# Another order of the operations in each step of a two-layer Mamba scan, on all four compute engines

## What is computed

```python
for i in range(2):
    u = layernorm(h)
    z, xBC, dt = split(u @ in_w.T)                 # 512, 640, 8
    dt = softplus(dt + dt_bias)
    xh, Bm, Cm = split(silu(causal_conv4(xBC)))    # 512, 64, 64
    state = exp(dt * A) * state + (dt * x_t) * B_t # scan over time, 8 heads
    y = state @ C_t + D * xh
    y = rmsnorm(y * silu(z)) @ out_w.T
    h = y + h
```

## Time and profile before

| | |
|---|---|
| median of 3 runs | 1979.9 us (1978.9 to 1980.2) |
| span of the profiled execution | 1980.0 us |
| PE busy | 1819.1 us, 92% |
| DVE busy | 1534.9 us, 78% |
| ACT busy | 1260.0 us, 64% |
| POOL busy | 1189.5 us, 60% |
| granted PE clock, mean over the span | 0.969 of full |

### The profile page before, as it was taken

One profiled execution on the slowest core, in us unless ns is written; L12 is line 12 of the kernel. 1 busy time (PEld: TensorE's weight loads), 2 busy tenths in 40 slices (PEclk: granted clock), 3 DMA queues, 4 the chain that ended last, 5 costly groups with the idle time before them and its releaser, 6 DMA issues. The chain is left out here.

```text
span 1980.0 us, 36525 instructions
## 1 busy us (share of the span) xinstructions
PE 1819.1 (92%) x12544; PEld 1380.2 (70%) x12544; DVE 1534.9 (78%) x3311; ACT 1260.0 (64%) x2221; POOL 1189.5 (60%) x1032
## 2 busy tenths in 40 slices
PE   5899999999999999999999999999974798988898
PEld 4577776777777777677777776777753677777776
DVE  4777888878778877777777777777635799999986
ACT  3677767776777666777677767777720455555554
POOL 2566666667666655555555555555540687868785
PEclk8899999999999989999999999999985899999999
DMA  4011111111111101111111111110005202012001
GB/s 141 22 39 38 39 48 58 37 42 37 37 37 37 48 28 49 59 39 44 37 37 37 37 48 58 37 42 26 28 11 148 86 1 95 34 41 89 33 12 43
DMA packets 87271, 91.96 MB, mean 46 GB/s; under 512 B 4928, under 2 KB 82448, under 8 KB 87184
## 3 DMA queue, kind: packets, MB, share of 16 engines
q1 hardware_dynamic: 79360, 79.46, 12.4%
q10 hardware_dynamic: 7824, 11.37, 2.3%
HBM read 57.26 MB, written 25.17 MB: 42 GB/s over the span
## 5 line engine op out<-in xcount | busy, mean ns | idle before, releaser
L860 POOL TENSOR_TENSOR L_xc<-L_xpad,L_vec 128x512 f32<-128x512 f32 x160 | 166.2, 1039 | 420.6 <-ACT L_xpad L659 401.3
L381 PE MATMUL L_front<-L_uhi,L_whi 128*128 128x512 f32 x576 | 247.2, 429 | 10.7 <-DVE L_xc L1078 7.3
L530 PE MATMUL L_mix<-L_wo,L_yg 128*128 128x256 f32 x1024 | 238.8, 387 | 3.2 <-POOL L_yg L852 3.2
L381 PE MATMUL L_front<-L_uhi,L_wlo 128*128 128x512 f32 x576 | 229.7, 399 | 0.0
L381 PE MATMUL L_front<-L_ulo,L_whi 128*128 128x512 f32 x576 | 229.7, 399 | 0.0
L1090 DVE TENSOR_TENSOR L_m<-L_dbank,L_gm 128x512 f32<-128x512 f32 x256 | 175.4, 685 | 69.6 <-ACT L_dbank L699 69.1
L530 PEld LDWEIGHTS L_mix<-L_wo,L_yg 128*128 128x128 f32 x1024 | 192.1, 193 | 35.0 <-issue 7.2
L852 POOL TENSOR_TENSOR L_yg<-L_yg,L_sz 128x512 f32<-128x512 f32 x128 | 164.3, 1284 | 85.9 <-DVE L_yg L1105 85.9
L659 ACT ACTIVATE L_xpad<-L_front,L_pbias 128x512 f32<-128x512 f32 x160 | 108.8, 681 | 131.8 <-PE L_front L381 130.9
L697 ACT ACTIVATE L_dbank<-L_dbank 128x512 f32<-128x512 f32 x256 | 148.8, 581 | 46.7 <-PE L_dbank L437 46.6
L1619 POOL TENSOR_TENSOR M_alo<-M_hT,M_ahi 128x512 fp32r<-128x512 f32 x96 | 125.6, 1312 | 75.1 <-DVE M_ahi L1681 75.1
(11 more groups left out here) (174 smaller groups left out, 4912.5 us busy)
## 6 DMA issues: line engine op xcount, KB each, us to landing
h<-L_hres SPq DMA_DIRECT2D x32, 512.0 KB, 3.0
L_hin<-in_x SPq DMA_DIRECT2D x16, 512.0 KB, 4.6
L_hres<-in_x SPq DMA_DIRECT2D x16, 512.0 KB, 3.8
L_cc<-L_xc ACTq DMA_DIRECT2D x64, 128.0 KB, 2.3
L_hin<-h SPq DMA_DIRECT2D x16, 512.0 KB, 4.7
L_hres<-h SPq DMA_DIRECT2D x16, 512.0 KB, 3.8
M_hin<-h SPq DMA_DIRECT2D x16, 512.0 KB, 6.4
M_xin<-in_x SPq DMA_DIRECT2D x16, 512.0 KB, 6.7
```

The source lines that it names most:

```text
L381: last = nc.tensor.matmul(to[:, :], ww[:, kd, tile * P:(tile + 1) * P], a[:, kd, :], start=i == 0, stop=i == len(passes) - 1)
L530: last = nc.tensor.matmul(mix[1 - s][:, (b % 2) * DM:(b % 2 + 1) * DM], yg[:, t, b * P:(b + 1) * P], wo[layer][:, t, :], start=t == 0, sto ...
L860: nc.gpsimd.tensor_tensor(xc[p][:, q, :].rearrange("p (b i) -> p b i", b=NB), xpad[:, q, :, 0:P], vector(layer, "conv_w", q * TAPS, 1).uns ...
```

## The change

The lines inside the four `step` functions change places. The instructions themselves, their waits and their buffers stay, with one exception: the wait for the cleared halo, which clear_halo did at once, is now done by the next set_halo that copies from it.

The hunks up to line 620 are PE's step, those from 749 to 802 ACT's, from 884 to 915 POOL's, and from 1169 on DVE's.

```diff
@@ -562,6 +562,6 @@
                     project_conv(n + 1, 0)
-                turn_x(n, p, 0)
+                decays(n, 4)
                 if more:
                     turn_dt(n + 1)
-                decays(n, 4)
+                turn_x(n, p, 0)
                 if follows_any(n):
@@ -571,5 +571,5 @@
                 turn_x(n, p, 1)
-                turn_x(n, p, 2)
                 decays(n, 5)
                 decays(n, 6)
+                turn_x(n, p, 2)
                 turn_x(n, p, 3)
@@ -587,9 +587,10 @@
                 outputs(n, p, 1)
-                outputs(n, p, 2)
                 if more:
                     project_conv(n + 1, 4)
-                    sum_da(n + 1)
                 new_state(n, 0)
-                new_state(n, 1)
+                outputs(n, p, 2)
+                if more:
+                    sum_da(n + 1)
                 outputs(n, p, 3)
+                new_state(n, 1)
                 if more:
@@ -600,5 +601,5 @@
                     project_z(n + 1, 3)
+                    scores(n + 1, 1 - p)
                     decays(n + 1, 0)
                     decays(n + 1, 1)
-                    scores(n + 1, 1 - p)
                 if more2:
@@ -606,5 +607,2 @@
                 result(n, layer, 0)
-                if more:
-                    decays(n + 1, 2)
-                    decays(n + 1, 3)
                 square_sums(n)
@@ -612,4 +610,8 @@
                     fold_bias(layer_of(n, layer, 2))
+                if more:
+                    decays(n + 1, 2)
                 if more2:
                     project_dt(n + 2)
+                if more:
+                    decays(n + 1, 3)
 
@@ -749,5 +751,4 @@
                     keep_dt(n + 1)
-                exp_decay(n, 3)
-                if more:
                     raw_conv(n + 1, layer1, 1 - p, 0)
+                exp_decay(n, 3)
                 exp_decay(n, 4)
@@ -757,2 +758,4 @@
                 exp_decay(n, 6)
+                if more:
+                    raw_conv(n + 1, layer1, 1 - p, 2)
                 keep_b(n)
@@ -761,4 +764,2 @@
                 exp_decay(n, 7)
-                if more:
-                    raw_conv(n + 1, layer1, 1 - p, 2)
                 exp_carry(n, 2)
@@ -766,5 +767,4 @@
                 if more:
-                    softplus(n + 1)
                     raw_conv(n + 1, layer1, 1 - p, 3)
-                    silu_conv(n + 1, layer1, 1 - p, 0)
+                    softplus(n + 1)
                 if more2:
@@ -772,21 +772,27 @@
                 if more:
-                    silu_conv(n + 1, layer1, 1 - p, 1)
-                    double_c(n + 1, 1 - p)
-                    silu_conv(n + 1, layer1, 1 - p, 2)
                     raw_conv(n + 1, layer1, 1 - p, 4)
+                    keep_halo(n + 1, 1 - p)
+                    silu_conv(n + 1, layer1, 1 - p, 0)
+                    double_c(n + 1, 1 - p)
+                    silu_conv(n + 1, layer1, 1 - p, 1)
                 square(n, 0)
-                square(n, 1)
-                square(n, 2)
                 if more:
+                    silu_conv(n + 1, layer1, 1 - p, 2)
                     silu_conv(n + 1, layer1, 1 - p, 3)
+                square(n, 1)
+                if more:
                     silu_z(n + 1, layer1, 0)
-                    keep_halo(n + 1, 1 - p)
+                square(n, 2)
+                if more:
                     silu_z(n + 1, layer1, 1)
-                    silu_conv(n + 1, layer1, 1 - p, 4)
                     silu_z(n + 1, layer1, 2)
                     silu_z(n + 1, layer1, 3)
-                    exp_decay(n + 1, 0)
                 square(n, 3)
                 if more:
-                    exp_decay(n + 1, 1)
+                    silu_conv(n + 1, layer1, 1 - p, 4)
+                    exp_sums(n + 1, 1 - p)
+                if starts_layer(n + 2):
+                    fold_weights(layer_of(n, layer, 2))
+                if more:
+                    exp_decay(n + 1, 0)
                 if more2:
@@ -794,6 +800,4 @@
                 if more:
+                    exp_decay(n + 1, 1)
                     exp_decay(n + 1, 2)
-                    exp_sums(n + 1, 1 - p)
-                if starts_layer(n + 2):
-                    fold_weights(layer_of(n, layer, 2))
 
@@ -883,3 +887,2 @@
                 twice = layer_of(n, layer, 2) == 0
-                decay_state(n, p)
                 if more:
@@ -887,5 +890,9 @@
                     first_tap(n + 1, layer1, 1 - p, 1)
-                to_end(n, p, 0)
+                if twice:
+                    model_norm(n + 2, p)
+                if more2:
+                    layer_norm(n + 2)
                 if more:
                     first_tap(n + 1, layer1, 1 - p, 2)
+                to_end(n, p, 0)
                 to_end(n, p, 1)
@@ -893,15 +900,10 @@
                     first_tap(n + 1, layer1, 1 - p, 3)
-                if more2:
-                    layer_norm(n + 2)
                 to_end(n, p, 2)
                 to_end(n, p, 3)
-                gate(n, 0)
                 if more:
                     first_tap(n + 1, layer1, 1 - p, 4)
+                decay_state(n, p)
+                gate(n, 0)
                 gate(n, 1)
-                if twice:
-                    model_norm(n + 2, p)
                 gate(n, 2)
-                if next_layer == 0:
-                    norm_residual(n + 1, c + p, 1 - p)
                 gate(n, 3)
@@ -909,6 +911,8 @@
                 add_squares(n, 2)
+                if next_layer == 0:
+                    norm_residual(n + 1, c + p, 1 - p)
                 add_squares(n, 3)
+                rsqrt(rrms, ssq, ss_done, n, rr_done)
                 if more:
                     second_operands(n + 1)
-                rsqrt(rrms, ssq, ss_done, n, rr_done)
 
@@ -1052,2 +1056,4 @@
                     dve.wait_ge(cleared, 1)
+                elif isinstance(n, int) and n % ITEMS < GROUPS:
+                    dve.wait_ge(halo_cleared, (n // ITEMS - 1) * GROUPS + g + 1)
                 nc.vector.tensor_copy(xpad[:, :, :, 0:HALO].rearrange("p q b i -> p (q b) i"),
@@ -1059,3 +1065,2 @@
                 nc.vector.memset(halo[g][:, :, :, :], 0.0).then_inc(halo_cleared, 1)
-                dve.wait_ge(halo_cleared, n // ITEMS * GROUPS + g + 1)
 
@@ -1169,2 +1174,4 @@
                 chunk2 = 0 if ends_sequence(n) else c + 1
+                if more:
+                    set_halo(n + 1, 1 - p)
                 if more2:
@@ -1172,13 +1179,11 @@
                 if more:
-                    set_halo(n + 1, 1 - p)
+                    convolve(n + 1, layer1, 1 - p, 0, 0)
                 weigh(n, 3)
-                scale_x(n, p, 0)
                 if more:
+                    convolve(n + 1, layer1, 1 - p, 0, 1)
                     bias_dt(n + 1, layer1)
-                    convolve(n + 1, layer1, 1 - p, 0, 0)
                 weigh(n, 4)
-                if more:
-                    convolve(n + 1, layer1, 1 - p, 0, 1)
                 if follows_any(n):
                     finish(n - 1, layer_of(n, layer, -1), None, 1 - p, 1)
+                scale_x(n, p, 0)
                 if more:
@@ -1204,20 +1209,22 @@
                     convolve(n + 1, layer1, 1 - p, 2, 1)
-                skip(n, layer, p, 0)
-                if more:
-                    finish_dt(n + 1, layer1, 1 - p)
                     convolve(n + 1, layer1, 1 - p, 2, 2)
                     convolve(n + 1, layer1, 1 - p, 3, 0)
+                skip(n, layer, p, 0)
+                if more:
                     convolve(n + 1, layer1, 1 - p, 3, 1)
-                    convolve(n + 1, layer1, 1 - p, 3, 2)
                 skip(n, layer, p, 1)
                 if more:
-                    split_sums(n + 1)
+                    finish_dt(n + 1, layer1, 1 - p)
+                    convolve(n + 1, layer1, 1 - p, 3, 2)
                     convolve(n + 1, layer1, 1 - p, 4, 0)
-                skip(n, layer, p, 2)
-                if more:
                     convolve(n + 1, layer1, 1 - p, 4, 1)
                     convolve(n + 1, layer1, 1 - p, 4, 2)
+                    split_sums(n + 1)
+                skip(n, layer, p, 2)
+                if more:
                     decay_operands(n + 1)
-                    first_operands(n + 1)
+                skip(n, layer, p, 3)
                 add_state(n, p, 0)
+                if more:
+                    first_operands(n + 1)
                 add_state(n, p, 1)
@@ -1225,3 +1232,2 @@
                     clear_halo(n, p)
-                skip(n, layer, p, 3)
                 if more:
@@ -1229,5 +1235,2 @@
                     weigh(n + 1, 0)
-                    weigh(n + 1, 1)
-                if starts_layer(n + 2):
-                    fold_rows(layer2)
                 if more2:
@@ -1237,3 +1240,5 @@
                 if more:
-                    weigh(n + 1, 2)
+                    weigh(n + 1, 1)
+                if starts_layer(n + 2):
+                    fold_rows(layer2)
```

(19 more changed lines are left out.)

22 lines of the change are left out of this document (10 added, 12 removed).

## The result

The changed kernel takes **1990.1 us** (1989.7 to 1991.6, four runs) against 1980.1 us for the kernel before in the same session: ratio 1.0051, 95% interval 1.0037 to 1.0065. The forecast was 1989. The profiled execution has a span of 1987.8 us, 7.8 more than before; its run took 1989.7, so a run's time lies 1.9 above its span. The text ahead of the prediction, and the prediction with it, set a span beside a median of run times and found 0.1 between them. Like with like, the profiled execution of the kernel before was a long one: 21 later runs of it had spans of 1975.6 to 1979.5, median 1977.7, against its 1980.0. So the change costs 10.1 us by the medians, where two traces show 7.8 and the prediction added up 9.3.

What follows compares the result with a forecast made beforehand. PE was taken as nearly the bound (42.96 of 44 us busy), paying for DVE's chain. Plain steps -0.5 - 0.6 + 1.3 = +0.2, times 29 = +5.8; start-up +2.0, layer change +1.5: +9.3 on 1980.0, 1989 us, range 1975 to 1997.

Steps and rivals of the forecast that it cites:

- After outputs, -0.5: Plain step, outputs to turn_cum: PE's 0.62 us wait before turn_cum goes, splitting new_state costs 0.1; sum -0.5 us.
- turn_cum to square_sums, -0.6: Plain step: decays 2 and 3 leave this stretch (0.53 us) and scores' move saves one switch; sum -0.6 us.
- Square sums to outputs, +1.3: Plain step, DVE chain: weigh 2 +0.60, set_halo held by second_operands +0.68, moments +0.4, less 0.4 us; sum +1.3.
- The moments' hold: One of moments' nine small DVE operations is held by POOL's first_tap 0: +0.4 us, bounds 0 and 1.04.
- the sentence in bold: Of the DVE chain from square sums to outputs: "Whatever is put into that chain, PE pays for.".
- My first rival: Second hold does not bite: chain +0.8 instead of +1.3, a step -0.3 us, 1976 us; chance 0.27.
- The wait before outputs: PE's 0.27 us idle before outputs waits for weigh 7, the end of the long DVE chain from the square sums.
- Start-up step, +2.0: bias_dt falls later on DVE, so project_conv 1 starts later: +2.0 us, bounds 1.0 and 4.0.
- Change of layer, +1.5: ACT rounds new weights earlier, delaying mean_square; fold_bias's wait grows from 1.33 to about 2.8: +1.5 us, bounds 0 and 3.
- Last step, 0: No next item to prepare; its waits on finish and second_operands trade places: 0 us.
- The cover that I called thin: With decay_state ahead on POOL, gates and add_squares end about 0.5 us before square_sums needs them: no cost.
- longer still: Rival: rsqrt 0.3 us later makes decays 4 wait for second_operands, 0.3 more a step, 1998 us; chance 0.12.

Runs made afterwards that it cites:

- 4: The kernel before with only the change's last third of a step (from outputs to turn_cum): 1962.6 us, ratio 0.9914.
- 6: 4 with new_state in two pieces, placed as in the changed kernel: 1964.2 us, ratio 0.9927.
- experiment 2: The changed kernel with set_halo done one step earlier, between mean_square and finish: 1978.7 us, ratio 0.9997.
- 3: The changed kernel with weigh 2 and the earlier set_halo between mean_square and finish, and weigh 3 ahead of convolve(0, 0): 1988.7 us, ratio 1.0047.
- 11: The changed kernel with moments ahead of set_halo again and weigh 3 ahead of convolve(0, 0): 1979.8 us, ratio 1.0002.
- experiment 10: The changed kernel with only moments and set_halo swapped back on DVE, moments first: 1992.3 us, ratio 1.0062.
- 7: The changed kernel with bias_dt back ahead of convolve(0, 0) on DVE and fold_weights back behind exp_decay 2 on ACT: 1989.2 us, ratio 1.0050.
- experiment 8: The changed kernel with the order of before from outputs to turn_cum on all four engines: 2026.4 us, ratio 1.0238.
- experiment 1: The changed kernel with weigh 2 back ahead of finish on DVE, nothing else: 1994.9 us, ratio 1.0079.

## Why the prediction was right, and where its reasons were not

The waits and holds that it named are in the rows. Several sizes were off, the account of the middle third left out a term, and the total came closer than its parts.

- **After outputs, -0.5**: measured -0.40 (13.72 to 13.32). The wait, 0.66 as a mean, is gone; what PE pays for it was mis-sized, some 0.25 in place of 0.1 (experiments 4 and 6: taking the wait away brings 0.55, the split takes 0.15 back).
- **turn_cum to square_sums, -0.6**: -0.57. But "scores ahead of decays 0 and 1 saves one switch" was wrong: the two together take 1.52 us, 1.42 before.
- **Square sums to outputs, +1.3**: +1.37 and +1.24. weigh 2 and set_halo's hold are in the rows with the predicted sizes, and convolve(1, 0) came at t = 25.09 (24.95 predicted). The moments' hold was mis-sized: 0.85 in the step shown where +0.4 was counted, because first_tap 0 started at t = 17.51 and not 17.1. What hid it is that the moments' nine operations began at 17.49 and not 17.7, and the ninth ended at 19.30, where the sum gives 19.05. What failed is the sentence in bold, that PE pays for whatever is put into that chain, as the account of it all. With 0.65 of the chain taken out (experiment 2) this third is still 18.78, +0.87. Decays 2 and 3 left the first third, which I counted as -0.6, and came into this one with their 0.53 us and the switches around them, which I counted nowhere. PE's own work in this third, its length less the idle time, is 18.55 there against 17.68 before, and 18.4 to 18.5 in experiments 3 and 11 with the same order on PE: +0.75 to +0.9. The third stood only 0.6 to 0.85 us above that in the changed kernel. My first rival's +0.8 would have made the third 18.7, 0.15 to 0.3 above what PE alone takes; the kernel that came nearest to it (experiment 2) ended at the time of before, not at 1976.
- **The wait before outputs**, which the prediction called the end of that chain, is 0.22 to 0.24 us as a mean over the inner steps of each of the fourteen kernels, also where the chain's head was 0.65 us shorter. So something behind convolve(0, 0) sets its length; which wait it is, no run separates.
- **The holds** explain where DVE's time goes, yet taking both away by the swap wins nothing (experiment 10), since convolve(0, 0) needs first_tap 0 in any case. The same 0.6 us are won by what is put into that time (11) or by an earlier set_halo (2).
- The Trainium skill's rule ("SBUF — State Buffer", "Who interferes with whom") agrees with the rows of after, 0.73 and 1.01 us, and with the held operations of the experiments. It doesn't agree with the COPY beside an rsqrt that took 0.19 us, shown under the hardware; there the measurement decides.
- **Start-up step, +2.0**: +3.1 (46.51 to 49.59), inside its bounds; project_conv 1 waited 3.35 us for bias_dt (the first row below). Undoing it gave 2.3 back (7). The 0.6 for a fall of PE's clock is a term that no run shows: the mean granted clock of this step was 0.88, against 0.85 before.
- **Change of layer, +1.5**: +1.0; fold_bias waited 2.55 us (2.8 predicted), the second row:
```profile
76.53 0.56 PE L381 MATMUL L_front<-L_uhi,L_whi 128*128 128x512 f32 x1 [3.35 <-DVE L_dtraw L997]
735.68 7.81 PE L353 MATMUL L_ybank<-L_vec,L_raw 128*128 128x1 f32 x36 [2.55 <-DVE L_ssq L1125]
```
- **Plain steps, +5.8**: the 29 together +8.3. The excess lies where the terms above were mis-sized.
- **Last step, 0**: from the last turn_cum to the last store it is 54.06 in place of 58.46 us, -4.4. The mean granted clock of this stretch is 0.91, against 0.85 before, and PE's busy time in it 46.3 against 48.8 us; the causes of the rest aren't separated.
- **The total**: the steps between the marks cost 12.4 us more, 9.3 were forecast. The trace of after is also 1.2 longer ahead of the first turn_cum and, behind the last one, 4.4 shorter in the last step and 1.4 in the MLP, where I had counted nothing. The trace of before has the longest such tail of all fourteen (554.4 us, the others 548.6 to 552.3). That the excess of the steps met a gain behind them, and the total so came out within 1.1 us, is in part luck.
- The wait for cleared halos and decay_state's place cost nothing that a PE row of the changed kernel shows. The cover that I called thin, POOL ahead of the square sums, was thin: experiment 8 lost 22 us to it, through norm_residual.
- The rival "longer still" did not come: decays 4 found second_operands ended (426.76 against 427.01), 0.25 us to spare.

## What to carry to other kernels

Take a change of order apart by stretches of the step before judging it: here one third was worth 16 us and the rest cost 24 (47 without the room that the third made for norm_residual), and the whole looked like a slight loss. Where work is moved off one stretch, book it at the place where it lands, on the engine that is nearly full, and add the neighbours' switches. And before an operation is moved, ask whether its old place kept two others apart: set_halo behind the moments did.

## What the runs showed of the hardware

- DVE operations of 4 to 60 elements a partition whose operands are all in SBUF (COPY, TENSOR_TENSOR, SCALAR_TENSOR_TENSOR, TENSOR_SCALAR; 0.16 to 0.20 us) take 0.5 to 1.1 us when a POOL operation of 512 or 1024 elements a partition runs, and end with it within 0.1 us, whichever of them is met (0.49 in experiment 1, 1.04 in 3, 1.10 in the earlier trace rows). The four bn_stats whose first half ran beside second_operands in experiment 2 took 1.40 us, as in the step of after, where they ran behind it.
- Not every POOL operation holds: in experiment 2 the COPY at 421.22 ran beside the rsqrt, in 0.19 us. Whether this is for its kind or for its 4 elements a partition, no run tells.
```profile
420.59 1.02 POOL L816 TENSOR_TENSOR L_rrms<-L_ssq,L_power 128x4 f32<-128x4 f32 x1 [1.77 <-DVE L_ssq L1125]
```
- A single bf16 matmul among fp32 ones costs PE some 0.1 us on either side: from the last matmul of project_dt over decays 3 to the second of project_conv 0 it takes 0.99 us with decays 3 in between, where the two matmuls without it took 0.47 in the kernel before; so 0.52 for one, against 0.53 for the pair of the earlier trace rows. The two kinds differ in type, in rows (64 and 128) and in the bank they write; no run separates these.
```profile
424.77 0.40 PE L368 MATMUL L_front<-L_uhi,L_wlo 128*8 128x512 f32 x1
425.10 0.39 PE L437 MATMUL L_dbank<-L_dmov,L_dstat 64*128 64x512 bf16 x1
425.42 0.50 PE L381 MATMUL L_front<-L_uhi,L_whi 128*128 128x512 f32 x1
425.76 0.39 PE L381 MATMUL L_front<-L_ulo,L_whi 128*128 128x512 f32 x1
```
